# A graph transformer on one NeuronCore: layers written out, upper halves of weights by ScalarE, and the order at the seams of attention and MLP

## What is computed

```python
h = maximum(layernorm(x), 0)
for i in range(4):
    y = cond_layer_norm(h, cond, s1[i], b1[i])           # scale and bias from a 16-wide condition
    q, k, v = y@wq[i]+bq[i], y@wk[i]+bk[i], y@wv[i]+bv[i]  # 4 heads of 128
    a = edge softmax of q[src].k[dst] over the edges of each src
    h = h + segment_sum(a * v[dst], src) @ wo[i] + bo[i]
    y = cond_layer_norm(h, cond, s2[i], b2[i])
    h = h + relu(y@m_w1[i]+m_b1[i]) @ m_w2[i] + m_b2[i]
x = x + h
x = x + gcn(relu(gcn(relu(layernorm(x)), W1)), W2)
```

## Time and profile before

| what | us |
|---|---|
| median of three runs | 2082.96 (2081.45 to 2086.16) |
| the profiled execution, its own time | 2087.25 |
| its span | 2085.4 |
| mean granted clock of TensorE | 0.973 |
| layer 0's projection starts | 203.59 |
| layer 1's, 2's and 3's projection starts | 626.59, 1034.62, 1437.90 |
| the convolutions' first product | 1843.04 |

### The profile page before, as it was taken

How to read it: one execution, slowest core, us unless ns; L and a number is a source line. 1 busy time by engine, 2 the same in 40 slices (tenths; PEclk the granted TensorE clock), 3 DMA queues, 4 the chain that set the end, 5 groups by cost and what they waited for, 6 DMA issues and landing times.

```text
span 2085.4 us, 35195 instructions
## 1 busy us (share of the span) xinstructions
PE 1943.0 (93%) x11664; PEld 1595.1 (76%) x11664; DVE 1357.2 (65%) x2790; ACT 772.9 (37%) x1515; POOL 523.4 (25%) x601
## 2 busy tenths in 40 slices
PE   5898997999989999999898999999989999899999
PEld 2455877888769888888797888878978988775543
DVE  6887556878764477887554788875558888650111
ACT  2212454555322255553223555532235554240000
POOL 1000243112371421124524113064142121610000
PEclk8899998999999999999999999999999999999999
DMA  4122453110301111112001111020012103310000
GB/s 129 24 48 57 142 157 96 34 34 25 110 7 46 58 35 34 37 45 87 22 31 58 35 45 47 29 81 31 31 50 66 34 24 106 82 49 0 0 20 30
DMA packets 50714, 108.22 MB, mean 52 GB/s; under 512 B 18143, under 2 KB 18195, under 8 KB 50608
## 3 DMA queue, kind: packets, MB, share of 16 engines
q1 hardware_dynamic: 50608, 106.87, 17.6%
HBM read 83.60 MB, written 23.25 MB: 51 GB/s over the span
## 4 chain that ended last, share of the span: by engine, by line
PE 75%; DVE 5%; issue 4%; DMA 2%; ACT 2%; POOL 1%; SPq 1%; DVEq 0%; POOLq 0%; ACTq 0%
PE ps L1393 54%; PE ps L1484 9%; PE ps L1613 4%; PE ps L1593 4%; PE ps L1413 2%; PE ps L1606 2%; PE ps L1402 1%; DVE pbuf L1103 1%; DMA ztmp<-in_x_dram 1%; SPq L265 1%; DVE PT L1119 1%; ACT b_rows L667 0%; DMA bt<-edge_bias_scratch 0%; POOL lnS L501 0%; ACT c_rows L669 0%
## 5 line engine op out<-in xcount | busy, mean ns | idle before, releaser
L1393 PE MATMUL ps<-kT,qg 128*125 128x512 f32 (+1 forms) x1440 | 320.7, 368 | 19.5 <-DVE nmx L1103 9.8
L1103 DVE CUSTOM_DVE_ANT_0 pbuf<-ps,bt 125x1250 f32<-125x1250 f32 x160 | 233.3, 1458 | 142.7 <-PE ps L1484 120.6
L1393 PEld LDWEIGHTS ps<-kT,qg 128*125 128x125 f32 x1440 | 250.7, 191 | 88.4 <-DVE nmx L1103 28.9
L1393 PE MATMUL ps<-PT,V 125*128 125x250 f32 x2400 | 313.7, 284 | 0.0
L762 ACT ACTIVATE PT<-ps 125x500 fp32r<-125x500 f32 (+1 forms) x480 | 214.7, 519 | 233.6 <-PE ps L1484 233.6
L1393 PEld LDWEIGHTS ps<-PT,V 125*128 125x128 f32 x2400 | 290.2, 190 | 0.4
L756 ACT ACTIVATE pbuf<-pbuf,nmx 125x1250 f32<-125x1250 f32 x160 | 214.8, 1343 | 198.3 <-DVE nmx L1103 198.3
L1119 DVE TENSOR_TENSOR PT<-ps,PT 125x500 fp32r<-125x500 f32 (+1 forms) x480 | 253.0, 582 | 5.7 <-ACT PT L762 5.7
L1484 PE MATMUL ps<-ident,pbuf 125*125 125x125 f32 x1600 | 208.7, 279 | 23.7 <-DVE PT L1119 20.7
L1484 PEld LDWEIGHTS ps<-ident,pbuf 125*125 125x125 f32 x1600 | 193.2, 194 | 26.6 <-DVE PT L1119 17.1
L523 POOL CAST qg<-qc 128x250 fp32r<-128x250 f32 x80 | 46.4, 580 | 490.6 <-PE ps L1393 476.3
(11 more groups left out here) (189 smaller groups left out, 2754.4 us busy)
## 6 DMA issues: line engine op xcount, KB each, us to landing
bt<-edge_bias_scratch SPq DMA_DIRECT2D x40, 546.9 KB
q_scratch<-qc SPq DMA_DIRECT2D x16, 500.0 KB, 2.6
qc<-q_scratch SPq DMA_DIRECT2D x16, 500.0 KB, 4.8
counts_scratch<-cblk SPq DMA_DIRECT2D x10, 546.9 KB
c_rows<-counts_scratch SPq DMA_DIRECT2D x10, 546.9 KB
edge_bias_scratch<-b_rows SPq DMA_DIRECT2D x10, 546.9 KB
counts<-counts_scratch SPq DMA_DIRECT2D x10, 546.9 KB
wm<-in_L_gnn_wo_dram SPq DMA_DIRECT2D x4, 1024.0 KB, 8.7
```

What stands on the lines that cost most here:

```text
L1103: v.tensor_tensor_reduce(out=P[:, u, :], in0=ps_S, in1=bt[:, u, :], scale=-1.0, scalar=FLOOR, op0=ALU.add, op1=ALU.min, accum_out=nmx[:, u ...
L1393: e = mm(out_, lhs(a), rhs(b), start=start and i == 0, stop=stop and i == 2)
```

## The change

- The layer loops of all five engines and the chunk loops of the MLP on TensorE and ScalarE are written out; `attn_rest` and `attn_first` for the first group too.
- The upper halves of the next layer's `wa` are made by ScalarE (`split_next`) behind `h_out` of chunks 0 to 2; GpSimd's `split_wa` keeps the subtraction. In the last layer ScalarE does it behind chunk 1.
- GpSimd's `split_ln` and `cond_chunk` of chunk 3 go behind `h_low` of its second half.
- In the first attention group TensorE attends to head 0's first half before unit 2, and waits for `WOS` after the group; VectorE takes the lower halves before the normalisations there.
- At the end of attention `turn_y` goes ahead of `attn_project`, with VectorE's and ScalarE's steps for it ahead of theirs for the projection and the MLP weights; the first MLP chunk waits for the adds bank by bank.
- In the last layer SyncE loads the last x tiles before W2 and the first six counts tiles.

```diff
@@ SyncE, layer(): the last layer's loads
                     load_x(range(8))
-                    load_w(W2[:, :, :], g_W2, "ldG")
-                    for t in range(6):
-                        move(counts[t], counts_dram[t * T:(t + 1) * T, :], "g_cnt")
                 sp.wait_ge(s["zB"], AHEAD + (2 * NC * (l + 1)))
...
                     load_x(range(8, NT))
+                    load_w(W2[:, :, :], g_W2, "ldG")
+                    for t in range(6):
+                        move(counts[t], counts_dram[t * T:(t + 1) * T, :], "g_cnt")
...
-            with sp.Fori(1, L - 1) as l:
+            for l in range(1, L - 1):
@@ GpSimd
-            def split_wa(raw, l, n, i, loads=64, parts=1):
+            def split_wa(raw, l, n, i):
-                pool.wait_ge(s["ldA"], 64 * l + loads)
+                pool.wait_ge(s["wa_hi"], 3 * l + n + 1)
                 settled(pool)
-                step = KD // parts
-                for k in range(0, KD, step):
-                    e = g.tensor_copy(wa[:, i, 0, k:k + step], raw[:, i, k:k + step])
-                e.then_inc(s["wa_hi"], 1)
-                pool.wait_ge(s["wa_hi"], n + 1)
-                settled(pool)
-                for k in range(0, KD, step):
-                    e = g.tensor_tensor(wa[:, i, 1, k:k + step], ...)
+                for k in range(KD):
+                    e = g.tensor_tensor(wa[:, i, 1, k], raw[:, i, k], wa[:, i, 0, k].bitcast(F32), ALU.subtract)
                 e.then_inc(s["wa"], 1)
...
                         cond_chunk(2 * NC * l + NC + c + 2, c + 2)
-                    elif c + 2 == NC and not last:
+                    h_low(l, c, (2, 3))
+                    if c + 2 == NC and not last:
                         split_ln(2 * l + 2)
                         cond_chunk(2 * NC * (l + 1), PROJECTED[0])
-                    h_low(l, c, (2, 3))
...
-            with pool.Fori(0, L - 1) as l:
+            for l in range(L - 1):
@@ ScalarE
+            def split_next(l, n, i, loads):
+                act.wait_ge(s["ldA"], 64 * (l + 1) + loads)
+                act.wait_ge(s["wmS"], 2 * l + 2)
+                sc.activation(wa[:, i, 0], wa_raw[:, i], ACT.Copy).then_inc(s["wa_hi"], 1)
...
+                yT_out(f2)
                 split_m(l)
                 if last:
                     for c in range(NC):
-                        yT_out(f2 + c)
+                        if c:
+                            yT_out(f2 + c)
...
                         h_out(l, c)
+                        if c == 1:
+                            split_next(l, 0, 0, 32)
...
-                    with act.Fori(0, NC) as c:
-                        yT_out(f2 + c)
+                    for c in range(NC):
+                        if c:
+                            yT_out(f2 + c)
                         rsqrt0(f2 + c + 1)
                         h_out(l, c)
+                        if c < 3:
+                            split_next(l, c, 2 - c, 64)
...
-            with act.Fori(1, L - 1) as l:
+            for l in range(1, L - 1):
@@ VectorE, layer()
                 score_max(l * NC, U + 1, 1, True)
...
+                turn_low(U, 0, 0)
                 normalise(U + 1, 1)
-                attn_first(l, 0, False)
+                score_max(l * NC, U + 2, 0, False)
+                turn_low(U + 1, 0, 1)
+                normalise(U + 2, 0)
+                score_max(l * NC, U + 3, 1, False)
+                normalise(U + 3, 1)
...
                 front_norm(f2, 0)
+                front_mod(f2)
                 out_low(l * NC + NC - 1, H - 1)
-                front_mod(f2)
+                yT_low(f2)
                 split_m(l, 0)
                 attn_add(l, NC - 1)
-                yT_low(f2)
                 split_m(l, 1)
...
-            with dve.Fori(1, L - 1) as l:
+            for l in range(1, L - 1):
@@ TensorE
-                features(ps_q, wmS[:, 0], yT, "h_mm", f, ("zC", 2 * a))
+                features(ps_q, wmS[:, 0], yT, "h_mm", f, ("zC", 2 * a) if c else ("zB", 2 * NC * (l + 1)))
...
-            def attn_rest(G, last):
+            def attn_rest(G, last, begun=False):
                 for k in range(2, UNITS):
-                    unit(G, k, last)
-                    attend(G, k // 2 - 1, k % 2)
+                    if begun and k == 2:
+                        attend(G, 0, 0)
+                        unit(G, k, last)
+                    else:
+                        unit(G, k, last)
+                        attend(G, k // 2 - 1, k % 2)
...
                 pe.wait_ge(s["v_e"], AHEAD + 2 * NC * (l + 1))
                 settled(pe)
+                attn_rest(l * NC, False, True)
                 pe.wait_ge(s["woS"], l + 1)
                 settled(pe)
-                with pe.Fori(0, NC - 1) as g_:
+                attn_first(l * NC + 1)
+                with pe.Fori(1, NC - 1) as g_:
...
                 attend(l * NC + NC - 1, H - 1, 2)
+                turn_y(2 * NC * l + NC)
                 attn_project(l * NC + NC - 1)
-                turn_y(2 * NC * l + NC)
-                pe.wait_ge(s["zB"], AHEAD + 2 * NC * (l + 1))
-                settled(pe)
-                with pe.Fori(0, NC - 1) as c:
+                for c in range(NC - 1):
                     mlp(l, c, 2 * l + 1)
...
-            with pe.Fori(0, L - 1) as l:
+            for l in range(L - 1):
```

More of the change, by code:

```diff
@@ L475, in _ @@
             pool.wait_ge(s["consts"], CONSTS)
-            def split_wa(raw, l, n, i, loads=64, parts=1):
-                n = 3 * l + n
-                pool.wait_ge(s["ldA"], 64 * l + loads)
+            def split_wa(raw, l, n, i):
+                pool.wait_ge(s["wa_hi"], 3 * l + n + 1)
                 settled(pool)
-                step = KD // parts
-                for k in range(0, KD, step):
-                    e = g.tensor_copy(wa[:, i, 0, k:k + step], raw[:, i, k:k + step])
-                e.then_inc(s["wa_hi"], 1)
-                pool.wait_ge(s["wa_hi"], n + 1)
-                settled(pool)
-                for k in range(0, KD, step):
-                    e = g.tensor_tensor(wa[:, i, 1, k:k + step], raw[:, i, k:k + step], wa[:, i, 0, k:k + step].bitcast(F32), ALU.subtract)
+                for k in range(KD):
+                    e = g.tensor_tensor(wa[:, i, 1, k], raw[:, i, k], wa[:, i, 0, k].bitcast(F32), ALU.subtract)
                 e.then_inc(s["wa"], 1)
@@ L618, in layer @@
                     if 0 < c < 4 and not (last and c > 1):
-                        split_wa(wa_raw, l + 1, c - 1, 0 if last else 3 - c, 32 if last else 64, KD)
+                        split_wa(wa_raw, l + 1, c - 1, 0 if last else 3 - c)
             for i in range(2):
                 pool.wait_ge(s[f"cnt_out{i}"], NT * 16)
-            with pool.Fori(0, L - 1) as l:
+            for l in range(L - 1):
                 layer(l, False)
@@ L739, in h_out @@
                 for j in range(KD):
-                    act.wait_ge(s["h_mm"], KD * (l * NC + c) + (j | 1) + 1)
+                    if j % 2 == 0:
+                        act.wait_ge(s["h_mm"], KD * (l * NC + c) + j + 2)
+                        settled(act)
                     for o, name in ((hT[:, 0, j, :], "hhi"), (qc[:, j, :], "hraw")):
@@ L1149, in unit, with attn_first @@
                     normalise(UNITS * G + n, n % 2)
-            def attn_first(l, g_, before):
+            def attn_first(l, g_):
                 for k in range(2):
                     unit(l * NC + g_, k, False)
-                    if before and k == 0:
+                    if k == 0:
                         out_low(l * NC + g_ - 1, H - 1)
-                if before:
-                    attn_add(l, g_ - 1)
+                attn_add(l, g_ - 1)
             def attn_rest(l, g_, last):
@@ L1219, in layer @@
                     edge_bias(NT - 1)
+                turn_low(U, 0, 0)
                 normalise(U + 1, 1)
-                attn_first(l, 0, False)
+                score_max(l * NC, U + 2, 0, False)
[3 more added lines that the diff above has]
+                normalise(U + 3, 1)
                 with dve.Fori(0, NC - 1) as g_:
                     attn_rest(l, g_, False)
-                    attn_first(l, g_ + 1, True)
+                    attn_first(l, g_ + 1)
                 attn_rest(l, NC - 1, True)
```

## The result

| what | before | after |
|---|---|---|
| median (runs), us | 2082.24 (2081.45 to 2086.16, four) | 2067.19 (2065.17 to 2070.26, four) |
| ratio of the medians, 95% interval | | 0.9925 [0.9907, 0.9943] |
| profiled execution / its span | 2087.25 / 2085.4 | 2065.17 / 2063.0 |
| mean granted clock | 0.973 | 0.977 |
| MLP starts, layers 0 to 3 | 545.72, 954.18, 1361.52, 1763.48 | 536.92, 940.16, 1339.53, 1744.08 |

Faster by 0.75%, or 15 us, where 33 were forecast: 2067.2 stands just outside the range. The profiled execution of before, 2087.25, was slower than all four of its runs and that of after was the fastest of its own, so the two traces differ by 22.4; what follows sums to that.

A forecast was written before the change was run, and what follows sets the result against it. TensorE, busy 93% of the span, bounds the kernel; only its stops and the slow clock after them can be won. Terms sum to -33.5: profiled 2087.25 to 2053.8, as a median 2049.5, about 2050 us; range 2032 to 2067.

The forecast's parts named there:

- part 3: GpSimd's h_low before split_ln, layers 0 to 2: -16.0 in chunk 3, +12.3 in chunk 4 from work pushed back.
- layer 3's chunk 2: Last layer's MLP, x tiles loaded first: chunk 2 falls from 21.15 to 17.35, -3.8.
- part 5: Attention start: WOS wait moved, -7.7 in layer 0; reordered first group, -5.1 over layers 1 to 3; together -12.8.
- rival D: Attention start wins nothing outside layer 0, and VectorE, slowed by WOS work, takes half of that: 2059, 11%.
- the jumps: TensorE's two jumps back, before layers 1 and 2, written out: 5.7 each with slow clock, -11.4.
- rival E: TensorE doesn't wait for the jump back; the 3.86 stays as a wait for VectorE's last add: 2061, 5%.
- the halves by ScalarE: ScalarE makes next wa's upper halves, GpSimd loses the cast; MLP chunk 2 falls to 13.27 in layers 0 to 2: -12.2.
- rival C: ScalarE's copy in MLP chunk 0 comes late, its loads landing late; wait and dip in three layers, +14: 2064, 8%.
- attention's end: turn_y ahead of the projection: +1.1 and a clock dip of +1.5 a layer, +10.4 over four layers.
- rival F: Attention loops no longer stay resident, so TensorE fetches at inner jumps: +46, 2096, slower than before; 4%.
- the rule of the Trainium skill: A taken branch outside two pages of 256 instructions stalls for a fetch; the attention loop would stall at every jump.
- the forecast's 1.5 for every such wait: Slow clock after every TensorE wait of 2.2 us or more, worth about 1.5 to 1.7 us; 1.5 at attention's end.

The follow-up runs named there:

- e12: The kernel after with one wait ahead of split_wa, for GpSimd's own bias adds (last layer: its adds of x): 2046.09 us, ratio 0.9826 to the kernel before.
- e3: The kernel after with TensorE's and VectorE's first-group order at attention start as before, WOS wait still behind the group: 2067.69 us, ratio 0.9915 to before.
- e7: e5 with TensorE's and VectorE's order in the first attention group as before (as in e3): 2032.51 us, ratio 0.9741 to the kernel before.
- e10: The kernel before with one edit, TensorE's wait for WOS moved behind the first attention group: 2078.98 us, ratio 0.9981 to the kernel before.
- e2: The kernel after with the end of attention as before (projection, then turn_y): 2053.78 us, ratio 0.9848 to the kernel before.
- e8: e5 with TensorE's layers 0 to 2 as a hardware loop again: 2038.22 us, ratio 0.9780 to the kernel before.
- e4: The kernel after with TensorE's layers 0 to 2 as a hardware loop again: 2072.47 us, ratio 0.9938 to the kernel before.
- e5: The kernel after with e1's earlier subtractions and e2's old end of attention together: 2029.29 us, ratio 0.9742 to the kernel before.
- e1: The kernel after with GpSimd's subtractions for the next wa one chunk earlier, last layer's ScalarE copy likewise: 2037.64 us, ratio 0.9784 to the kernel before.
- e11: The kernel after with the subtraction's slices written k:k + 1 as in the kernel before: 2065.60 us, ratio 0.9923 to the kernel before.
- e9: The kernel before with one edit, h_low of chunk 3 ahead of split_ln and cond_chunk: 2086.35 us, ratio 1.0014 to the kernel before.

## Why the prediction failed by half

Two steps failed, by 6.5 and 7.1 us. The first is the +12.3 of part 3. I gave chunk 4 "the period of that chunk, 17.35", because the same subtraction met the same VectorE steps in chunk 2 of before. Measured: 20.5, 17.8 and 20.3, together +18.8. The meeting was foreseen, and its time was right: GpSimd ended the subtraction 6.8 us into chunk 4, as said. Not foreseen was that VectorE would be shut out for the whole of it: in chunk 2 of before the subtraction followed a cast and a gap of 0.18, and with the cast gone it follows the bias add with none. e12 gives the gap back and chunk 4 falls to 16.05. Removing an instruction also removed the gap behind it. The hold also took layer 3's chunk 2 to 18.2 where 17.35 was said (-3.0 in place of -3.8).

The second is part 5, -12.8 said and -5.7 measured. For layer 0, -7.7 was said and -6.7 came. For layers 1 to 3 I had -5.1 and got +1.0; e3 and e7 put the whole reordering at 0. I had "the 2.0 us of attend moved forward fill the 1.83, and the 1.0 comes new"; the 1.0 came (0.82) and the 1.83 stayed, one unit later. This is rival D without its other half, which e10 rules out.

A third thing, 2.4 us, had no term at all: chunk 0 takes 2.4 more in four layers, waiting 0.39 for hT and 0.60 for y. With the end undone (e2) the 0.39 is gone and chunk 0 takes 949.93 - 935.40 = 14.53 in place of 15.04; the 0.59 stays, and its cause is open.

Right, and by their own reasons: the jumps (-11.4 said, -11.4 by distances, 8.9 by e8; in after TensorE waits for nothing at the two seams: rival E falls), though in the changed kernel, with chunk 4 standing still ahead of them, undoing the part cost only 5.3 (e4); the halves by ScalarE (-12.2 said, -12.7), with its copies covered (rival C falls); chunk 3 (-16.0 said, -16.1); attention's end (+10.4 said, +8.8 by distances; e2's 13.4 includes what it took from chunk 0), through the wait of 2.9 that came as 3.04. With full clock the order costs 20.36 - 19.48 = 0.9 a layer, for 1.1 said; the rest is slow clock. No inner loop stalled (rival F falls), as before, so the rule of the Trainium skill (Runtime: NRT & Kernel Launch, "Instruction fetch mechanics") that the forecast weighed has no support in the trace for TensorE's loop of 596 instructions.

Summed by terms: 6.5 from chunk 4, 7.1 from the attention start, 2.4 and 0.8 from the chunks 0 and layer 3, less 1.6 of the end, 3.0 ahead of attention and 0.6 in chunks 2 and 3, is 11.6: the profiled execution took 2065.17 where 2053.8 was said. The other 6 of the 17.7 that the median is off are the runs' own scatter: before's profiled execution lay 5 above its median, after's 2 below. A forecast that starts from one execution, 5 us above the median, should have had that in its range.

The fastest version is e5, 2029.3, with e7 not distinguishable from it by ratio: everything in the change but the new end of attention, with the subtractions one chunk earlier.

## What to carry to other kernels

GpSimd work that is off the critical path still has to be put where VectorE works on PSUM or is idle (in e1, layer 0, the subtractions met VectorE's PSUM steps at 0.69 and 1.26 and its statistics at 1.28, the lengths they have elsewhere). Where it must meet VectorE's small SBUF steps, give its run a wait that really stops it: for its own last result, directly at the front or between the pieces. A wait that is already met leaves no gap: after's `split_wa` waits for `wa_hi`, and its row of 592.74 has none ahead of it. A step that is put behind another is a debt to the next chunk: follow the queue until it is empty, since moving h_low alone moved a wait and won nothing. And undo each part of a bundle by itself: here undoing one part won 13 us and undoing another changed nothing, both hidden in a result that looked good.

## What the runs showed of the hardware

- A VectorE instruction of 0.16 us took 6.10 to 6.44 us beside an unbroken run of GpSimd's two-input instructions, 15 times in five kernels (after, e2, e3, e4, e11), and no small step took more than 1.26 where a gap of about 0.2 stood directly ahead of the subtraction (before, e9, e12). Why is open. The Trainium skill (SBUF — State Buffer, "SBUF: two separate sides") says that the port pair the two engines share is an exclusive lock held for the whole instruction. The 1.21 of e12 agrees, one piece being 1.25; the 6.14 doesn't follow from it, being almost five of them.
- A jump back over one layer of TensorE's code was followed by a wait of 3.7 to 6.2 us and a slow first product (before, e8), and by one of 2.35 or 1.55 where the engine had stood still just ahead of it (e4). The slow product doesn't always come: in e9 and e10 the waits were 3.20 to 3.54 and the 48 matmuls behind them took 5.80 to 5.88.
- Waits of about 3 us didn't always bring the slow clock. In after, layer 1, 3.04 was followed by `turn_y` at 1.93 and a granted clock of 0.86 over 928 to 940, while in layer 1 of e1 and e12 the same wait, 3.02, was followed by 1.07 and a clock of 1.00 over 918 to 930. Why is open; the forecast's 1.5 for every such wait was too sure.
